# Routed experts write into seven DRAM regions of their own, summed on VectorE, in place of one accumulated region

## The chip, the core and the metric

The kernel runs on one NeuronCore of a Trainium2 chip. The metric is the device time of one execution in microseconds (us). The engines are TensorE (PE, matmuls; PEld its weight loads), VectorE (DVE), ScalarE (ACT), GpSimd (POOL) and SyncE (SP), each with its own queue of instructions, which it works off in order; they wait for one another on semaphores. SP issues plain DMAs. GpSimd issues the indirect ones, whose row numbers lie in a tile. All data is float32 unless a row says otherwise.

## The reference

Two transformer blocks on x of 8 batches x 512 tokens x 128 channels. Block 0 has attention and then a mixture of experts; block 1 has windowed attention and another feed-forward part. The change lies in the mixture of experts (`h` is the normalised, modulated x, `gb` a gate of batch and channel):

```
N = B * S                      # 4096 tokens
k = max(4, ceil(N * 2.0 / E))  # 1024 rows for each of E = 8 experts
xt = x.reshape(N, D)
scores = softmax(xt @ Wr)
G, idx = top_k(scores.T, k)    # per expert: the 1024 tokens that score highest
X_in = xt[idx]
h = gelu(einsum('ekd,edh->ekh', X_in, W1) + b1[:, None, :], approximate=False)
X_e = einsum('ekh,ehd->ekd', h, W2) + b2[:, None, :]
out = zeros((N, D)).at[idx.reshape(-1)].add((G[..., None] * X_e).reshape(E * k, D))
x = x + gb * out
```

A token may be chosen by several experts, so the sum over experts is part of the result. Within one expert every token stands at most once.

## The kernel before

**Stages.** The program has three: attention of block 0 (to about 459 us), the experts (function `moe`, to about 713) and block 1. X, the running activations, stays in SBUF as 32 tiles of 128 tokens. Attention leaves in DRAM `d_tab` (a token's 128 normalised channels and its 8 scores) and `d_hT` (the transposed rows).

**Expert 0 is dense.** It computes all 4096 tokens in four chunks of 1024 and weighs each token with its score or zero (`gate0`). Experts 1 to 7 are routed. The order is `ITS = (0, 0, 0, 1, 2, 3, 4, 5, 6, 7, 0)`: three dense chunks, the routed experts, the last dense chunk. `rx` is the expert's number less 1, `LOOP = 3`, `NR = 7`.

**Threshold search.** While TensorE computes the first dense chunks, VectorE searches in 15 rounds for the score above which an expert has 1024 tokens. From it VectorE and TensorE make the row numbers: `onehot(rx)` (L1377 to L1386) writes a comparison matrix R on VectorE, `lists(rx)` (L1461) multiplies it out on TensorE, and `index(rx)` (L1391 to L1395) writes `idx`. Two experts are done ahead; the others are made two experts ahead inside the loop (`AHEAD = 2`), at the top of VectorE's turn.

**One routed expert.** GpSimd gathers 1024 rows of `d_tab` into XG by eight indirect DMAs of 128 rows (L1280). TensorE transposes them (L1469, `rows_T`), ScalarE copies them to XT, TensorE computes the first layer (L1482, 16 instructions), ScalarE applies gelu (L1614), TensorE the second layer (L1494), ScalarE copies and adds the bias (OT, L1623), TensorE transposes back (L1501, `outputs_T`, two groups of four), and VectorE multiplies by the scores into Y (L1427, two of them, h = 0 and 1). GpSimd scatters Y by eight indirect DMAs (L1290) into `d_acc`, adding to what is there. Since two experts may add to one row, the scatters of an expert wait until those of the expert before have landed (L1286). On GpSimd's queue stands gathers of rx + 2, scatters of rx, gathers of rx + 3 and so on.

**TensorE's order in a turn.** First layer of expert e (with `outputs_T` of the expert before, h = 1, inside it), `lists` for the expert two ahead (it waits for R), `rows_T` of the next expert, `gates` (L1531, three small products with the gates of one batch; VectorE copies them at L1435 to L1438), second layer, `outputs_T` of e, h = 0. The second layer overwrites the PSUM banks that VectorE's Y reads.

**Dense outputs.** ScalarE leaves the outputs of a dense chunk in YD (L1627). TensorE transposes them (L1511, `dense_outputs_T`) and VectorE adds them, times `gate0`, to X (L1411, `dense_outputs`). For the first three chunks this stands behind expert 7: six groups of four transposes in turn with six groups of four updates, since both halves share two PSUM banks.

**End of the stage.** SP waits for the last scatter to land and loads the first two batches of `d_acc` into AC (L1850, 256 KB each). VectorE's `first_rows` multiplies AC by the gate GG and adds it to X (L1839, L1840), takes the statistics, adds the last dense chunk, and drains. GpSimd, after its wait for the scatters, drains (L1301), takes the root (L1846, L1847), and VectorE begins block 1 with bxn (L2076). The other batches of `d_acc` are loaded and added on GpSimd in block 1 (L2205, L2206). `d_acc` was cleared by one DMA of 2 MB during attention (L1086), from `zrow`.

## Time and profile before

| | us |
|---|---|
| median of 3 runs | 979.48 (976.18 to 981.32) |
| the profiled execution | 979.78 |
| its span in the profile | 978.0 |
| TensorE busy | 824.1 (84%) |
| VectorE busy | 572.1 (58%) |
| ScalarE busy | 440.4 (45%) |
| GpSimd busy | 413.9 (42%) |
| mean granted clock of TensorE | 0.904 of full speed |

The profile is of one execution, and its times in rows count from the start of the span. Shares are means over three stages that differ; in the stage of the experts each engine has idle time that some other engine ends. A row of a timeline says start, duration, engine, line, operation, output <- inputs, shapes and count, and in brackets how long the engine was idle before and what ended that. PE's rows overlap a little, since matmuls are pipelined and their ends are modelled.

### The profile page before, as it was taken

What the parts mean: (1) busy time and instruction counts of PE and PEld (TensorE: products, weight loads), DVE (VectorE), ACT (ScalarE), POOL (GpSimd) and SP (SyncE); (2) the same over time, 40 slices, a digit from 0 to 9 for tenths busy, and PEclk for the clock granted to TensorE, in tenths of its full rate; (3) what the DMA queues carried; (4) which work ended last, traced back from release to release, by engine and by line L of the source; (5) the groups of instructions that cost most, each with busy time, mean ns of one, the idle gap of its engine ahead of it and who ended that gap; (6) DMA issues with size and microseconds to landing.
All of it is one profiled execution on the core that took longest, in us unless ns stands there. A gap on an engine that the chain in (4) does not pass through costs nothing.

```text
span 978.0 us, 16352 instructions
## 1 busy us (share of the span) xinstructions
PE 824.1 (84%) x5918; PEld 400.0 (41%) x5918; DVE 572.1 (58%) x1480; ACT 440.4 (45%) x710; POOL 413.9 (42%) x539
## 2 busy tenths in 40 slices
PE   4687999899898989895888999789856679999885
PEld 3223333343333333333343454334434346666554
DVE  3676676657676767635677333300486567777741
ACT  1003554445454545471323433333246567776641
POOL 6221012323232322030005688887535676885323
PEclk9657999889999999996899998889968899999987
DMA  4211344134433132122101232333300111111100
GB/s 126 67 42 34 86 129 96 36 99 139 98 59 97 55 98 60 43 87 87 44 0 35 43 45 43 45 44 34 48 22 1 23 23 24 34 24 24 33 13 22
DMA packets 69095, 52.89 MB, mean 54 GB/s; under 512 B 20624, under 2 KB 62040, under 8 KB 68440
## 3 DMA queue, kind: packets, MB, share of 16 engines
q1 hardware_dynamic: 59160, 44.28, 17.6%
q0 software_dynamic: 9856, 7.58, 5.6%
q8 instruction: 48, 0.79, 0.3%
q14 instruction: 31, 0.25, 0.1%
HBM read 31.76 MB, written 18.23 MB: 51 GB/s over the span
## 4 chain that ended last, share of the span: by engine, by line
PE 50%; DVE 17%; POOL 13%; issue 8%; DMA 6%; ACT 3%; SPq 1%; POOLq 1%; DVEq 0%; ACTq 0%
PE bank L404 8%; POOL d_acc L1290 7%; PE bank L387 7%; DVE MX L793 6%; PE ps_s L362 5%; POOL XG L1280 3%; PE b1ps L1946 3%; PE b1ps L1935 3%; PE bank L407 2%; PE ps_s L371 2%; PE b1ps L1908 2%; PE ps_o L1494 2%; PE b1ps L1959 2%; DMA Q<-d_q 2%; PE ps_h L1482 1%
## 5 line engine op out<-in xcount | busy, mean ns | idle before, releaser
L793 DVE TENSOR_REDUCE MX<-bank 128x1 f32<-128x512 f32 (+3 forms) x352 | 216.2, 638 | 85.9 <-PE bank L407 81.6
L578 ACT ACTIVATE PR<-ps_s 128x1024 f32<-128x1024 f32 x160 | 158.9, 1023 | 155.5 <-PE ps_s L371 89.9
L404 PE MATMUL bank<-K,Q 96*128 96x512 bf16 (+3 forms) x512 | 136.4, 327 | 31.5 <-DVE MX L793 16.6
L404 PEld LDWEIGHTS bank<-K,Q 96*128 96x128 bf16 x512 | 44.5, 102 | 153.8 <-DVE MX L793 112.9
L362 PE MATMUL ps_s<-Q,K 99*128 99x512 bf16 x320 | 97.4, 393 | 1.8 <-DMA Q<-d_m 1.8
L1290 POOL DMA_INDIRECT d_acc<-Y,idx x56 | 87.6, 1565 | 20.3 <-issue 16.5
L407 PE MATMUL bank<-maskT,identb 128*128 128x128 bf16 (+2 forms) x352 | 92.7, 263 | 0.0
L1494 PE MATMUL ps_o<-H,w 128*128 128x512 f32 x176 | 91.5, 672 | 0.0
L387 PE MATMUL bank<-PR,VE 128*32 128x512 f32 x640 | 90.4, 639 | 0.0
L1280 POOL DMA_INDIRECT XG<-d_tab,idx x56 | 54.0, 965 | 77.6 <-DVE idx L1395 61.2
L1614 ACT ACTIVATE H<-ps_h,b1T 128x512 f32<-128x512 f32 x88 | 60.4, 687 | 42.2 <-PE ps_h L1482 40.0
L919 POOL TENSOR_SCALAR ve<-mv 128x4 f32<-128x4 f32 x8 | 1.9, 234 | 177.0 <-DVE mv L658 177.0
L1427 DVE TENSOR_TENSOR Y<-ps_o,XG 128x512 f32<-128x512 f32 x14 | 9.7, 692 | 99.0 <-PE ps_o L1501 81.8
L2058 ACT ACTIVATE PT<-b1ps 128x512 f32<-128x512 f32 x64 | 38.2, 597 | 39.6 <-PE b1ps L1946 38.5
L1482 PE MATMUL ps_h<-XT,w 128*128 128x512 f32 x112 | 54.0, 606 | 0.6 <-ACT XT L1606 0.5
L1494 PEld LDWEIGHTS ps_o<-H,w 128*128 128x128 f32 x176 | 36.6, 215 | 42.7 <-issue 42.0
L2063 ACT ACTIVATE PB<-SU 128x512 f32<-128x512 f32 x64 | 40.1, 627 | 19.6 <-DVE SU L2125 19.3
L2194 POOL TENSOR_SCALAR bxn<-X,bmv,brs 128x128 f32<-128x128 f32 x56 | 47.7, 864 | 1.5
L1935 PE MATMUL b1ps<-KB,QT 64*32 64x512 f32 x512 | 36.6, 629 | 13.2 <-issue 9.2
L2125 DVE TENSOR_TENSOR SU<-b1ps,mxs 128x512 f32<-128x512 f32 x64 | 44.2, 691 | 2.2
L889 POOL TENSOR_SCALAR xn<-X,mv,rs 128x128 f32<-128x128 f32 x56 | 44.0, 801 | 1.5
L1946 PE MATMUL b1ps<-ident,PB 128*128 128x128 f32 x256 | 43.3, 293 | 0.0
(333 smaller groups left out, 1388.8 us busy)
## 6 DMA issues: line engine op xcount, KB each, us to landing
Q<-d_q SPq DMA_DIRECT2D x24, 384.0 KB
d_q<-qs SPq DMA_DIRECT2D x24, 128.0 KB, 2.3
X<-L_attn_x SPq DMA_DIRECT2D x8, 256.0 KB, 4.7
w<-L_ffn_W SPq DMA_DIRECT2D x8, 256.0 KB, 3.5
d_acc<-zrow SPq DMA_DIRECT2D x1, 2048.0 KB, 9.4
w<-L_ffn_W SPq DMA_DIRECT2D x1, 2048.0 KB, 9.4
AC<-d_acc SPq DMA_DIRECT2D x8, 256.0 KB, 2.8
y<-X SPq DMA_DIRECT2D x8, 256.0 KB, 2.3
```

Source lines behind the costliest of these rows:

```text
L362: last = nc.tensor.matmul(ps_s[half][:, 512 * hh:512 * hh + 512], K[b % QB][0:KM, P * i:P * i + P], Q[b % QB][0:KM, 4 * hg:4 * hg + 4, P * ...
L387: last = nc.tensor.matmul(ps_y[32 * j:32 * j + 32, :], VE[b % QB][:, i, :], PR[t % 2][:, j, :], start=(i == 0), stop=(i == g), tile_positi ...
L404: nc.tensor.matmul(ps_mx[G % 2][:, x * w:(x + 1) * w], Q[b % QB][0:KR, h, P * g:P * g + P], K[b % QB][0:KR, 0:w], start=(x == 0), stop=Fal ...
L407: nc.tensor.matmul(diag, identb[:, :], bc(maskT[:, :].unsqueeze(1), [P, len(hs), P]), start=False, stop=True, skip_group_check=True).then_ ...
L578: nc.scalar.activation(PR[t % 2][:, 2 * half:2 * half + 2, :], ps_s[half][:, :].rearrange("p (a f) -> p a f", a=2), ACT.Exp, scale=DH ** - ...
L793: nc.vector.tensor_reduce(MX[b % 2][:, c:c + len(hs)], ps_mx[G % 2][:, 0:len(hs) * w].rearrange("p (x w) -> p x w", w=w), AX_X, ALU.max).t ...
L1280: nc.gpsimd.indirect_dma_start(out=XG[rx % 4][:, k, :], out_offset=None, in_=g.d_tab, in_offset=bass.IndirectOffsetOnAxis(ap=idx[:, rx + 1 ...
L1290: nc.gpsimd.indirect_dma_start(out=g.d_acc, out_offset=bass.IndirectOffsetOnAxis(ap=idx[:, rx + 1, k:k + 1], axis=0), in_=Y[rx % 2][:, k, ...
L1482: T_.matmul(ps_h[u % 2][:, :], g.w1[:, e, P * c:P * c + P], rows[:, 512 * h:512 * h + 512], start=True, stop=True).then_inc(h_ps, 1)
L1494: last = T_.matmul(ps_o[h][:, :], g.w2[:, ITS[it], c, :], H[h][:, c, :], start=(c == 0), stop=(c == NC_DI - 1))
L1935: last = T_.matmul(ps_s[(U + hh) % SB][32 * j:32 * j + 32, :], QT[b % 2][64 * hh:64 * hh + 64, q:q + 32], KB[b % 2][64 * hh:64 * hh + 64, ...
L1946: last = T_.transpose(ps_t[:, P * k:P * k + P], PB[U % 3][:, P * k:P * k + P], ident[:, :])
```

## The change

**Regions.** `d_acc` and its clearing in attention go. There are seven DRAM tensors `d_reg[0..6]` of 2 MB, cleared in a row by SP at the start of the expert stage, behind the loads of the dense chunks. The scatters of rx write `d_reg[rx]` with no add, and wait for no other expert's scatters; the first waits for the clearing. Their semaphore is split into two, for even and odd rx.

**Sums.** `part[b]`, one per batch, is made of free SBUF space (YD of the first three chunks and XD[2]). SP loads region 0 straight into it once its scatters have landed. For regions 1 to 5 it loads 256 KB at a time into the two buffers of AC, and VectorE adds each to `part[b]` (`add_region`); `sum_rd` counts the adds and frees the buffer. `add_region(rx - 1)` stands at the end of VectorE's turn rx, for rx of 2 to 6. Behind the last turn `add_sums` multiplies each part by GG and adds it to X, eight times two operations. Region 6 takes the path of `d_acc`: it is the one that `first_rows` and GpSimd add.

**Dense outputs.** Since YD is needed, the transposes and updates of the first three dense chunks move from behind expert 7 to before expert 1, on TensorE and on VectorE; the counts of the semaphores follow.

```diff
-    d_acc = dram("d_acc", [NB * T, D], F32)
+    d_reg = [dram(f"d_reg{i}", [NB * T, D], F32) for i in range(NE - 1)]
...
-                    if n == 0:
-                        sp.dma_start(d_acc.rearrange("(i p) d -> p i d", p=P),
-                                     bc(zrow[:, :].unsqueeze(1), [P, NTILE, D])).then_inc(s_lw, 16)
...
-    g.d_acc = d_acc
+    g.d_reg, g.d_acc = d_reg, d_reg[NE - 2]
...
+    part = [YD[:, T * b:T * b + T] for b in range(2 * LOOP)] + [XD[2][:, 0:T], XD[2][:, T:2 * T]]
+
+    def scattered(eng, rx):
+
+        eng.wait_ge(scat[rx % 2], 16 * NS * (rx // 2 + 1))
...
         def scatters(rx):
-            if rx >= 1:
-                pool.wait_ge(scat, 16 * NS * rx)
+            if rx == 0:
+                pool.wait_ge(zeroed, 16 * NR)
             for k in range(NS):
                 if k % 4 == 0:
-                    pool.wait_ge(y_rdy, 2 * rx + k // 4 + 1)
-                nc.gpsimd.indirect_dma_start(out=g.d_acc, out_offset=bass.IndirectOffsetOnAxis(ap=idx[:, rx + 1, k:k + 1], axis=0),
-                                             in_=Y[rx % 2][:, k, :], in_offset=None,
-                                             compute_op=ALU.add).then_inc(scat, 16)
+                    pool.wait_ge(y_rdy, 2 * LOOP + 2 * rx + k // 4 + 1)
+                nc.gpsimd.indirect_dma_start(out=g.d_reg[rx], out_offset=bass.IndirectOffsetOnAxis(ap=idx[:, rx + 1, k:k + 1], axis=0),
+                                             in_=Y[rx % 2][:, k, :], in_offset=None).then_inc(scat[rx % 2], 16)
...
+        def add_region(rx):
+            if rx == 1:
+                dve.wait_ge(first_in, 16 * NB)
+            for b in range(NB):
+                k = NB * (rx - 1) + b
+                dve.wait_ge(sum_in[k % 2], 16 * (k // 2 + 1))
+                if rx >= 2:
+                    dve.wait_ge(sum_rd, k - NB + 1)
+                V.tensor_tensor(part[b], part[b], g.AC[k % 2][:, :, :].rearrange("p i d -> p (i d)"), ALU.add
+                                ).then_inc(sum_rd, 1)
+
+        def add_sums():
+            dve.wait_ge(sum_rd, NB * (NR - 2))
+            for b in range(NB):
+                p3 = part[b].rearrange("p (i d) -> p i d", d=D)
+                lk(V.tensor_tensor(p3, p3, bc(g.GG[:, b:b + 1, :], [P, T // P, D]), ALU.mult))
+                Xb = g.X[:, T // P * b:T // P * b + T // P, :]
+                V.tensor_tensor(Xb, Xb, p3, ALU.add)
+
+        for c in range(LOOP):
+            dense_outputs(c)
...
             V.scalar_tensor_tensor(g.WVG[:, j, :], gate[2], 0.5, g.WT[:, 2, :], ALU.mult, ALU.mult).then_inc(gg_cp, 1)
+            if rx >= 2:
+                add_region(rx - 1)
+        add_sums()
         g.first_rows(dve)
...
         mix_weights_T()
+        for c in range(LOOP):
+            for h in range(2):
+                dense_outputs_T(c, h)
         for h in range(2):
             rows_T(0, h)
...
-        sp.wait_ge(scat, 16 * NS * NR)
+        for rx in range(NR):
+            sp.dma_start(g.d_reg[rx].rearrange("(i p) d -> p i d", p=P), bc(g.zrow[:, :].unsqueeze(1), [P, NTILE, D])
+                         ).then_inc(zeroed, 16)
+        for rx in range(NR - 1):
+            scattered(sp, rx)
+            for b in range(NB):
+                rows = g.d_reg[rx][T * b:T * b + T, :].rearrange("(i p) d -> p i d", p=P)
+                if rx == 0:
+                    if b == 0:
+                        sp.wait_ge(oT_ps, 2 * LOOP)
+                    sp.dma_start(part[b].rearrange("p (i d) -> p i d", d=D), rows).then_inc(first_in, 16)
+                    continue
+                k = NB * (rx - 1) + b
+                if k >= 2:
+                    sp.wait_ge(sum_rd, k - 1)
+                sp.dma_start(g.AC[k % 2][:, :, :], rows).then_inc(sum_in[k % 2], 16)
+        scattered(sp, NR - 1)
+        sp.wait_ge(sum_rd, NB * (NR - 2))
         g.first_loads(sp)
```

VectorE's queue at the turn of expert 3 and the start of the turn of expert 4, before. Y is expert 3's output, GG to WVG the gate copies, ohA to R the one-hot of expert 6, lst to idx its index:

```order
L1427 TENSOR_TENSOR Y<-ps_o,XG 128x512 [waits m_gathered2_1,m_out_transposed]
L1435 COPY GG<-ps_l 128x128 [waits p_gates_ps]
L1436 TENSOR_TENSOR WPG<-ps_l,w_proj 128x128
L1437 TENSOR_TENSOR BPG<-ps_l,b_proj 128x128
L1438 SCALAR_TENSOR_TENSOR WVG<-ps_l,WT 128x128
L1377 TENSOR_TENSOR ohA<-stile,kval 128x256
L1379 TENSOR_TENSOR A<-ohA,iota 128x32x8 [waits dve_chain]
L1380 TENSOR_SCALAR A<-ohA,iota_p 128x32x8
L1386 TENSOR_TENSOR R<-ps_r,slotf 128x4096 [waits m_list_ps,dve_chain]
```

The same place after, from the last gate copy on:

```order
L1460 SCALAR_TENSOR_TENSOR WVG<-ps_l,WT 128x128
L1427 TENSOR_TENSOR YD<-YD,AC 128x512 [waits m_region_rows0,m_first_region]
L1427 TENSOR_TENSOR YD<-YD,AC 128x512 [waits m_region_rows1]
L1427 TENSOR_TENSOR YD<-YD,AC 128x512 [waits m_region_rows0]
L1427 TENSOR_TENSOR YD<-YD,AC 128x512 [waits m_region_rows1]
L1427 TENSOR_TENSOR YD<-YD,AC 128x512 [waits m_region_rows0]
L1427 TENSOR_TENSOR YD<-YD,AC 128x512 [waits m_region_rows1]
L1427 TENSOR_TENSOR XD<-XD,AC 128x512 [waits m_region_rows0]
L1427 TENSOR_TENSOR XD<-XD,AC 128x512 [waits m_region_rows1]
L1381 TENSOR_TENSOR ohA<-stile,kval 128x256
L1383 TENSOR_TENSOR A<-ohA,iota 128x32x8 [waits dve_chain]
```

Eight adds, each with a wait for a load, now stand between the gate copies and the one-hot of expert 6. The same happens one turn later, for expert 7.

SP's queue of the same stage after; before, the loads of AC at the end came directly behind the dense loads (XD):

```order
L1679 DMA XD<-d_hT 128x1024 [waits a0_h_st]
L1681 DMA d_reg<-zrow 128x32x128 x7
L1690 DMA YD<-d_reg 128x4x128 [waits m_out_transposed,m_scattered0]
L1690 DMA YD<-d_reg 128x4x128 x5
L1690 DMA XD<-d_reg 128x4x128 x2
L1695 DMA AC<-d_reg 128x4x128 [waits m_scattered1]
L1695 DMA AC<-d_reg 128x4x128
L1695 DMA AC<-d_reg 128x4x128 [waits m_sums_read] x6
L1695 DMA AC<-d_reg 128x4x128 [waits m_sums_read,m_scattered0]
```

Of the eight loads of region 1 two are issued without a wait for an add; each of the other six waits for one. From region 2 on all eight do.

## Rows read from the trace of the kernel before

**Rows 1.** Page, costliest groups: count | busy us, mean ns | idle before, releaser.
```profile
L1290 POOL DMA_INDIRECT d_acc<-Y,idx x56 | 87.6, 1565 | 20.3 <-issue 16.5
L1427 DVE TENSOR_TENSOR Y<-ps_o,XG 128x512 f32<-128x512 f32 x14 | 9.7, 692 | 99.0 <-PE ps_o L1501 81.8
```
**Rows 2.** GpSimd's timeline: start us, duration us, line, operation [idle before].
```profile
546.12 0.94 POOL L1280 DMA_INDIRECT XG<-d_tab,idx  x1 [0.30 <-issue]
...
554.87 1.63 POOL L1290 DMA_INDIRECT d_acc<-Y,idx  x1 [0.31 <-issue]
556.81 1.57 POOL L1290 DMA_INDIRECT d_acc<-Y,idx  x1 [0.30 <-issue]
...
580.03 1.62 POOL L1290 DMA_INDIRECT d_acc<-Y,idx  x1 [0.30 <-issue]
```
**Rows 3.** Chain of waits at the end of the experts: start us, us, what.
```profile
701.65 3.30 DMA d_acc<-Y,idx
704.98 7.09 POOLq L1301
```
**Rows 4.** TensorE's timeline: first output transposes of experts 1 to 7, one list.
```profile
552.66 0.60 PE L1501 MATMUL ps_o<-ident,OT 128*128 128x128 f32 x4
...
573.84 0.60 PE L1501 MATMUL ps_o<-ident,OT 128*128 128x128 f32 x4
...
583.68 0.97 PE L1461 MATMUL ps_l<-A,R 128*128 128x16 bf16 x32 [1.44 <-DVE R L1386]
...
596.66 0.60 PE L1501 MATMUL ps_o<-ident,OT 128*128 128x128 f32 x4
...
644.20 0.60 PE L1501 MATMUL ps_o<-ident,OT 128*128 128x128 f32 x4
...
668.50 0.60 PE L1501 MATMUL ps_o<-ident,OT 128*128 128x128 f32 x4
...
684.67 0.60 PE L1501 MATMUL ps_o<-ident,OT 128*128 128x128 f32 x4
```
**Rows 5.** VectorE's and TensorE's timelines: dense updates, last chunk's first layer.
```profile
687.70 5.25 DVE L1411 SCALAR_TENSOR_TENSOR X<-ps_o,gate,X 128x128 f32<-128x128 f32 x20
...
692.88 8.60 PE L1482 MATMUL ps_h<-XD,w 128*128 128x512 f32 x16
```
**Rows 6.** VectorE's timeline at the end of the stage.
```profile
707.73 0.69 DVE L1839 TENSOR_TENSOR AC<-AC,GG 128x512 f32<-128x512 f32 x1 [4.46 <-DMA AC<-d_acc]
...
710.38 2.13 DVE L1411 SCALAR_TENSOR_TENSOR X<-ps_o,gate,X 128x128 f32<-128x128 f32 x8
713.68 3.08 DVE L2076 TENSOR_SCALAR bxn<-X,bmv,brs 128x128 f32<-128x128 f32 x4 [1.17 <-POOL brs L1847]
```
**Rows 7.** Clearing on the page; landings of AC's loads in the tile's view.
```profile
d_acc<-zrow SPq DMA_DIRECT2D x1, 2048.0 KB, 9.4
...
DMA to landing us min/median/max: 2.6/2.8/4.5
```
**Rows 8.** VectorE's timeline: one-hot preparation, the second Y, the one-hot.
```profile
512.84 0.42 DVE L1377 TENSOR_TENSOR ohA<-stile,kval 128x256 f32<-128x256 int32 x1
...
555.46 0.69 DVE L1427 TENSOR_TENSOR Y<-ps_o,XG 128x512 f32<-128x512 f32 x1 [1.46 <-PE ps_o L1501]
...
556.86 0.41 DVE L1377 TENSOR_TENSOR ohA<-stile,kval 128x256 f32<-128x256 int32 x1
...
558.03 4.42 DVE L1386 TENSOR_TENSOR R<-ps_r,slotf 128x4096 bf16<-128x4096 f32 x1
```
**Rows 9.** Windows, two second layers: stretch, us, busy by engine, PEclk, DMA, GB/s.
```profile
586.96:596.82 9.86, 9.86 (x19) 4.32 (x19) 0.00 (x0) 0.69 (x1) 8.03 (x7) 0.72 0.37 36
609.19:616.32 7.13, 7.13 (x19) 3.25 (x19) 0.00 (x0) 0.69 (x1) 6.18 (x4) 1.00 0.41 37
```
**Rows 10.** SP's timeline: the last two loads of dense chunks.
```profile
460.99 1.95 SPq L1654 DMA_DIRECT2D XD<-d_hT  x2
```
**Rows 11.** View of tile XG: duration min/median/max, first and last start.
```profile
L1280 POOL DMA_INDIRECT XG<-d_tab,idx x56: 940/947/1243, 521.0 to 654.3; - x56
```

39 lines of the change are left out of this document (18 added, 21 removed).

## The prediction

> **What bounds the kernel now.** I read the page first, then the GpSimd timeline of the expert stage, then the chain of waits, and last the VectorE and TensorE timelines of the same stretch. The page gives GpSimd 56 scatters at 1565 ns [rows 1]. The timeline shows them back to back with the 56 gathers: a gather every 1.25 us, a scatter with add every 1.86 us, and the first scatters of two experts 25.2 us apart (554.87 to 580.03) [rows 2], which is 8 x 1.25 + 8 x 1.86 = 24.9. The chain of waits passes through them and through the landing of the last scatter to 704.98, then through GpSimd's drain (7.09 us) [rows 3]. Call a turn the time from the first output transposes of one expert to those of the next. The six turns are 21.2, 22.8, together 47.5 for the next two, then 24.3 and 16.2, 132.0 in all [rows 4]. So the first two turns are TensorE's own pace; GpSimd's lag makes itself felt only in turns 4 and 5, where expert rows come late. The scatter is the bound of only part of the stage, and a gain must be read turn by turn.
>
> **What goes away.** A scatter without add is not in this trace. Its nearest rows are the gather (step 1.25) and the scatter with add (1.86) [rows 2]; I take 1.25, since it also writes 128 descriptors for 512-byte rows and reads nothing at its destination. That frees 56 x 0.61 = 34 us of GpSimd, and the wait for the scatters of the expert before goes too. Where GpSimd is no longer late it is worth nothing more: at 1.25 or at 1.86 the sum below moves by 1 us at most, in the tail. A turn without GpSimd's lag is TensorE's: 21.2 to 22.8 with a list, 17.1 without (16.2 [rows 4] and an estimated 0.9 for the eight transposes of rows that turn 6 has not).
>
> **Front: the dense transposes move.** Six groups of four transposes and the 24 updates of X stood after expert 7 and now stand before expert 1. VectorE's update sets their pace, 5.25 us for 20 [rows 5], 1.05 per group of four; the sixth group begins five such steps after the first and takes 0.5 to 1.1. Expert 1 therefore starts about 5.5 us later. At the old place they took as long between expert 7 and the last dense chunk; but there TensorE's gain buys nothing, since VectorE will be later (tail).
>
> **Middle: a wait stands ahead of the one-hot.** This is the large term. After experts 3 to 7 VectorE adds the region of the expert before: eight loads of 256 KB through two buffers, an add after each. VectorE works in order, and what is queued behind are the one-hot and the index of a later expert. TensorE waits for that one-hot before it goes on to the second layer.
> An add of 128x512 from SBUF is the 0.69 of the row on AC [rows 6], 0.72 with its start. A load takes 2.76 from its issue (704.97, the end of the chain's scatter) to VectorE's start at 707.73 [rows 3, 6]; the landings of such loads are 2.6, 2.8 and 4.5 at least, median and most [rows 7]. Two loads are in ahead. Load 3 is issued only when add 1 is done, about 0.1 later, so each further pair costs 0.1 + 2.76 + 0.69 = 3.55: a region takes 2 x 0.72 + 3 x 3.6 = 12.2. These rows come from a queue without scatters in it; beside gathers and scatters I take 3.0 instead of 2.76, hence r = 12.9 per region.
> Only the one-hots of experts 6 and 7 stand behind a region. In those two turns: 3.5 from the output transposes to the end of the second Y (552.66 to 556.15), 0.7 for gate copies, 12.9 for the region, 5.6 for the one-hot (556.86 to 562.45) [rows 4, 8], and from the list to the next output transposes 13.0 (583.68 to 596.66) [rows 4]. That last figure is a turn in which the clock had fallen after a wait: the second layer took 9.86 at a granted clock of 0.72, against 7.13 at 1.00 [rows 9]; after a wait of some 13 us I take the slow one. Sum 35.7, twice 71.4 against 47.5: **+23.9**.
> Turn 5 has no list: TensorE 17.1, VectorE 3.5 + 0.7 + 12.9 = 17.1, against 24.3: **-7.2**. Turn 6 stays 16.2 for TensorE, with VectorE 0.9 behind. Turns 1 and 2 keep their 44.0. Middle together +16.7.
>
> **Tail: VectorE ends last.** From the last expert's output transposes (684.67) to the first normalisation of the next stage (713.68) it is 29.0 now [rows 4, 6]. After: 2.5 to the end of both Y, 0.7 gate copies, 12.9 for the sixth region, 0.9 for the last gate copies, 16 operations of 0.72 for the gated sums = 11.5, then the part that stood there before, first rows 2.65 (707.73 to 710.38) and X updates 2.13 [rows 6], and 0.3 to the start: 33.6. TensorE's last chunk needs 8.6 for its first layer [rows 5] and 7.1 for the second [rows 9], near 20 with gates and transposes, and hides. GpSimd's drain of 7.09 [rows 3] hides too. Tail **+4.6**. If a scatter keeps 1.86, region 6 comes about 1 us later.
>
> **Zeroing.** One clearing of 2 MB (9.4 us to landing [rows 7]) leaves the attention stage, where no engine waits for it: at nothing, up to 1 us of gain. Seven are issued behind SP's last dense load, near 463 [rows 10], with nothing that is needed soon behind them on SP: 7 x 9.4 = 66 us, to 529. Their cover is the threshold search; they are needed at the first scatter, 554.87 + 5.5 = 560. The gathers of expert 1 start at 521 [rows 11] and share the last 8 us with them; TensorE now asks for those rows 5.5 later, which is their margin. Cost nothing; if the cover is gone, a few us (rival 4).
>
> **Sum.** 5.5 + 16.7 + 4.6 = 26.8. The profiled execution took 979.8 (span 978.0, 1.8 around it), 0.3 above the median of 979.5: 979.8 + 26.8 = **1006.6, forecast 1007**.
>
> **A rule against this change.** Around VectorE's one-hot preparation, which reads two SBUF tensors, GpSimd is in scatters: 0.41 beside them (556.86), 0.42 in a stretch without any (512.84) [rows 8]; the add of SBUF on SBUF should keep its 0.69. The Trainium skill, page "SBUF — State Buffer", section "Who interferes with whom", says that a VectorE instruction with two SBUF inputs contends with a GpSimd instruction that reads SBUF, and the later one blocks for all of the other's time. By that rule 40 adds beside gathers and scatters would wait; the trace's one pair of rows does not bear it out.
>
> **Rivals.**
> (1) Adds on time. If all loads of a region were in before VectorE asks, r = 8 x 0.72 = 5.8. The sum falls by three regions (turns 3, 4 and the tail; turns 5 and 6 are then TensorE's): 26.8 - 3 x 7.1 = 5.5, **985**. Against it: load 3 cannot be issued before add 1 is done.
> (2) The other side, faster: the region's sum fits in VectorE's idle time and nothing waits for it, with GpSimd's lag gone. Place: between gate copies and one-hot. With r = 0 the sum is 26.8 - 38.7 = -11.9, **968**. The sign turns at r = 12.9 - 26.8 / 3 = 4.0, that is 0.5 us for load and add together; the add alone measures 0.69. For it: VectorE idles 99 us before the 14 Y now [rows 1]. Against it: that idle time lies behind the one-hot, the sum stands before it.
> (3) Loads slowed by gathers and scatters. All five regions lie on the path then. Landings of 3.6 give r = 14.7 and +9, **1016**; 4.5 (the longest seen) gives r = 17.4 and +22, **1029**.
> (4) Zeroing collides. 14.7 MB keep the DMA engines full through the threshold search. If it takes more than 560 - 463 = 97 us, the first scatter waits; if gathers of expert 1 land after 539, TensorE does. Price 3 to 10: **1010 to 1017**.
> (5) Port lock. A GpSimd gather is under way for 0.94 of each 1.25 us [rows 2]; an add would wait 0.4 on average, four adds in series per region, five regions: +8, **1015**.
>
> **How the numbers follow.** Forecast 0.64, with its own spread: landings of 2.6 (-4), clock kept high in the two long turns (-3), front 5 to 6.5, landings of 3.3 (+5), so 998 to 1013. Rival 1 0.05, rival 2 0.03, rival 3 0.13, rival 4 0.07, rival 5 0.06; 0.02 for what I have not seen. 996 to 1024 leaves out rivals 1 and 2 and the far half of 3, about 0.16. A measurement of this kernel can tell about 0.5% (5 us) from no change: faster 0.04 (rival 2), within it 0.02, slower 0.94.
>
> **What would show it.** In the changed kernel: scatters at a step near 1.25; TensorE idle some 13 us before the lists of experts 6 and 7, ended by R; VectorE's adds in pairs, each second one after about 2 us of waiting for a load; turns of 35 to 36 twice, then 17 and 17; the X updates before expert 1, whose output transposes come near 558; the end of VectorE's part about 33 us after expert 7's. I am wrong if the adds follow each other without waits (rival 1), if the one-hots of experts 6 and 7 don't hold TensorE (rival 2), or if the adds are longer than 0.7 (rival 5).

## The result, and the profile after

The changed kernel took **1023.5 us** (1020.6 to 1030.3, 4 runs), beside 979.1 us of the kernel before: ratio 1.0465, 95% interval 1.0403 to 1.0527. Forecast were 1007 us in a range of 996 to 1024: the direction was right and the size too small, a ratio of 1.028 against 1.0465. In us the median lies at the upper edge of the range, as a ratio (1024 over 979.5 is 1.0454) just above it. The profiled execution took 1020.6 us, its span is 1018.8.

The page of the changed kernel (count | busy us, mean ns | idle before, releaser; at the end DMA issues, KB, us to landing) answers [rows 1] and [rows 7]:

```profile
L1284 POOL DMA_INDIRECT XG<-d_tab,idx x56 | 53.4, 953 | 134.8 <-DVE idx L1399 119.6
L1294 POOL DMA_INDIRECT d_reg<-Y,idx x56 | 56.8, 1015 | 36.8 <-DVE Y L1452 20.9
L1452 DVE TENSOR_TENSOR Y<-ps_o,XG 128x512 f32<-128x512 f32 x14 | 9.6, 691 | 64.5 <-PE ps_o L1524 44.8
d_reg<-zrow SPq DMA_DIRECT2D x7, 2048.0 KB, 17.4
AC<-d_reg SPq DMA_DIRECT2D x48, 256.0 KB, 2.9
```

A scatter without add holds GpSimd 1015 ns, as against 1565 in [rows 1]. (L1284 and L1294 are the gathers and scatters, L1452 is Y, L1524 the output transposes, L1486 the list.) TensorE's timeline (start us, us, engine, line, operation [idle before <- what ended it]) answers [rows 4], again with the first output transposes of experts 1 to 7 (L1524), and ahead of them the dense transposes (L1536) at their new place:

```profile
524.50 0.60 PE L1536 MATMUL ps_o<-ident,YD 128*128 128x128 f32 x4
531.36 1.12 PE L1536 MATMUL ps_o<-ident,YD 128*128 128x128 f32 x4 [6.26 <-issue]
537.36 2.15 PE L1536 MATMUL ps_o<-ident,YD 128*128 128x128 f32 x8 [4.88 <-DVE X L1415]
...
541.63 1.64 PE L1494 MATMUL ps_x<-ident,XG 128*128 128x128 f32 x8
...
560.74 0.60 PE L1524 MATMUL ps_o<-ident,OT 128*128 128x128 f32 x4
...
567.34 1.10 PE L1507 MATMUL ps_h<-XT,w 128*128 128x512 f32 x2 [2.13 <-ACT H L1639]
571.46 2.07 PE L1507 MATMUL ps_h<-XT,w 128*128 128x512 f32 x2 [3.02 <-issue]
575.01 3.78 PE L1507 MATMUL ps_h<-XT,w 128*128 128x512 f32 x4 [1.48 <-ACT H L1639]
...
588.75 0.60 PE L1524 MATMUL ps_o<-ident,OT 128*128 128x128 f32 x4
...
616.07 0.60 PE L1524 MATMUL ps_o<-ident,OT 128*128 128x128 f32 x4
...
639.38 1.02 PE L1486 MATMUL ps_l<-A,R 128*128 128x16 bf16 x32 [6.60 <-DVE R L1390]
...
653.12 0.60 PE L1524 MATMUL ps_o<-ident,OT 128*128 128x128 f32 x4
...
675.98 1.02 PE L1486 MATMUL ps_l<-A,R 128*128 128x16 bf16 x32 [14.46 <-DVE R L1390]
...
690.19 0.60 PE L1524 MATMUL ps_o<-ident,OT 128*128 128x128 f32 x4
...
707.23 0.60 PE L1524 MATMUL ps_o<-ident,OT 128*128 128x128 f32 x4
...
723.39 0.60 PE L1524 MATMUL ps_o<-ident,OT 128*128 128x128 f32 x4
```

The turns are 28.0 and 27.3, then 37.1 and 37.1, then 17.0 and 16.2. The two long ones have the length that was forecast. In the second TensorE waits 14.46 us for R. In the first it waits only 6.60, since its own first layer is late there, but VectorE's queue sets the length all the same. VectorE's timeline shows what TensorE waits for: the region's adds, at first in pairs with 2.3 to 2.4 us of waiting for a load between them, then one by one with shorter waits (three more adds in rows left out here), and the one-hot of expert 6 behind them:

```profile
620.69 1.29 DVE L1427 TENSOR_TENSOR YD<-YD,AC 128x512 f32<-128x512 f32 x2
624.26 1.49 DVE L1427 TENSOR_TENSOR YD<-YD,AC 128x512 f32<-128x512 f32 x2 [2.29 <-DMA AC<-d_reg]
628.16 0.69 DVE L1427 TENSOR_TENSOR YD<-YD,AC 128x512 f32<-128x512 f32 x1 [2.41 <-DMA AC<-d_reg]
...
633.72 0.42 DVE L1381 TENSOR_TENSOR ohA<-stile,kval 128x256 f32<-128x256 int32 x1
```

From 620.69 to 633.80, the end of the last add, a region takes 13.1. What was not forecast is the rest: 28.0 and 27.3 in the turns that should have kept their 44.0 together, and 35.1 us from the first one-hot (506.49) to the transposes of expert 1's rows (541.63), which had taken 19.7. ScalarE's and VectorE's timelines of that stretch say who waits:

```profile
523.38 0.78 ACT L1652 ACTIVATE YD<-ps_o,b2g,gbT 128x512 f32<-128x512 f32 x1 [7.42 <-remote]
530.53 0.78 ACT L1652 ACTIVATE YD<-ps_o,b2g,gbT 128x512 f32<-128x512 f32 x1 [6.38 <-remote]
533.35 0.49 ACT L1666 ACTIVATE WT<-ps_l 128x384 f32<-128x384 f32 x1 [2.04 <-remote]
```
```profile
521.94 0.17 DVE L1395 COPY lst<-ps_l 128x16 f32<-128x16 f32 x1 [3.87 <-remote]
...
536.18 2.16 DVE L1415 SCALAR_TENSOR_TENSOR X<-ps_o,gate,X 128x128 f32<-128x128 f32 x8 [12.70 <-remote]
```

All five read what TensorE writes, and all wait long after TensorE's row has ended: X starts at 536.18, although the first four transposes are recorded at 524.50 and the other four at 531.36. The profile sees the semaphore change at the moment of release, but no instruction that would have changed it ("remote"). I call these **delays**. The last such wait ends at 630.0; from the one-hot of turn 3 on the kernel runs as forecast.

### The profile page after: what moved, and what is told of

It is laid out like the page before. It is cut to its first block, busy times and chain, and to the rows that moved or that the text cites. A ratio compares the mean times of both kernels' runs of the same rounds, so it can differ in the third digit from the quotient of the medians.

```text
span 1018.8 us, 16497 instructions
## 1 busy us (share of the span) xinstructions
PE 818.5 (80%) x5918; PEld 398.9 (39%) x5918; DVE 609.0 (60%) x1536; ACT 440.5 (43%) x710; POOL 381.3 (37%) x539
## 3 DMA queue, kind: packets, MB, share of 16 engines
q0 software_dynamic: 3584, 7.58, 2.6%
## 4 chain that ended last, share of the span: by engine, by line
PE 48%; DVE 21%; issue 14%; DMA 8%; ACT 2%; POOL 2%; SPq 2%; another core or an unknown queue 2%; DVEq 0%; POOLq 0%; ACTq 0%
PE bank L404 7%; PE bank L387 7%; DVE MX L793 6%; PE ps_s L362 5%; DMA AC<-d_reg 3%; PE b1ps L1988 3%; PE ps_o L1517 3%; PE b1ps L1977 3%; PE bank L407 2%; PE b1ps L2001 2%; PE ps_s L371 2%; DMA Q<-d_q 2%; DVE R L1390 2%; PE b1ps L1950 2%
## 5 line engine op out<-in xcount | busy, mean ns | idle before, releaser
L404 PE MATMUL bank<-K,Q 96*128 96x512 bf16 (+3 forms) x512 | 133.6, 321 | 34.3 <-DVE MX L793 17.8
L1284 POOL DMA_INDIRECT XG<-d_tab,idx x56 | 53.4, 953 | 134.8 <-DVE idx L1399 119.6
L362 PE MATMUL ps_s<-Q,K 99*128 99x512 bf16 x320 | 94.8, 384 | 2.2 <-DMA Q<-d_m 2.2
L387 PE MATMUL bank<-PR,VE 128*32 128x512 f32 x640 | 88.0, 623 | 0.0
L1517 PE MATMUL ps_o<-H,w 128*128 128x512 f32 x176 | 85.6, 636 | 0.0
L1507 PE MATMUL ps_h<-XT,w 128*128 128x512 f32 x112 | 63.8, 689 | 17.3 <-ACT H L1639 12.3
L1294 POOL DMA_INDIRECT d_reg<-Y,idx x56 | 56.8, 1015 | 36.8 <-DVE Y L1452 20.9
L1452 DVE TENSOR_TENSOR Y<-ps_o,XG 128x512 f32<-128x512 f32 x14 | 9.6, 691 | 64.5 <-PE ps_o L1524 44.8
## 6 DMA issues: line engine op xcount, KB each, us to landing
d_reg<-zrow SPq DMA_DIRECT2D x7, 2048.0 KB, 17.4
```

Source lines behind the costliest of these rows:

```text
L362: last = nc.tensor.matmul(ps_s[half][:, 512 * hh:512 * hh + 512], K[b % QB][0:KM, P * i:P * i + P], Q[b % QB][0:KM, 4 * hg:4 * hg + 4, P * ...
L387: last = nc.tensor.matmul(ps_y[32 * j:32 * j + 32, :], VE[b % QB][:, i, :], PR[t % 2][:, j, :], start=(i == 0), stop=(i == g), tile_positi ...
L404: nc.tensor.matmul(ps_mx[G % 2][:, x * w:(x + 1) * w], Q[b % QB][0:KR, h, P * g:P * g + P], K[b % QB][0:KR, 0:w], start=(x == 0), stop=Fal ...
L1294: nc.gpsimd.indirect_dma_start(out=g.d_reg[rx], out_offset=bass.IndirectOffsetOnAxis(ap=idx[:, rx + 1, k:k + 1], axis=0), in_=Y[rx % 2][:, ...
L1507: T_.matmul(ps_h[u % 2][:, :], g.w1[:, e, P * c:P * c + P], rows[:, 512 * h:512 * h + 512], start=True, stop=True).then_inc(h_ps, 1)
L1517: last = T_.matmul(ps_o[h][:, :], g.w2[:, ITS[it], c, :], H[h][:, c, :], start=(c == 0), stop=(c == NC_DI - 1))
```

## What was tested

Theory at first (A): the seven clearings, 14.7 MB in the same stretch, cause the delays. Rival (B): the scatters without add. Each group below ran beside its own runs of the kernel before. Stretches are read from each profile: *front*, first one-hot to the first transposes of XG; turns as in the prediction; *tail*, expert 7's output transposes to TensorE's first ones of the next stage; *stage*, first one-hot to those. "Remote" counts idle stretches of ScalarE and VectorE between 500 and 760 us that the profile ends with that word.

```
kernel (group)                    time   before  remote  front  turns1+2  3+4   5     6     tail  stage
before (of the record)            979.8  979.5     0     19.7    44.0     47.5  24.3  16.2  32.2  202.9
before (3)                        983.8  981.2    11     18.5    45.1     50.8  17.0  16.2  35.1  205.1
changed (of the record)          1023.5  979.1    11     35.1    55.3     74.1  17.0  16.2  36.1  253.0
changed (2)                      1020.9  984.4     5     34.1    52.1     73.1  17.0  16.2  36.0  248.3
changed (4)                       999.2  977.0     0     23.4    44.0     74.5  17.0  16.2  36.4  230.1
changed (5)                      1004.9  978.3     0     23.4    44.0     74.0  17.0  16.2  36.1  229.4
clearings early (1)              1002.0  977.7     0     23.4    44.0     74.0  17.0  16.2  35.8  229.0
clearings early (3)              1025.0  981.2     5     25.1    55.6     73.3  17.0  16.2  36.3  245.6
sums behind the index (1)         974.6  977.7     0     25.1    45.6     45.4  17.0  16.2  35.8  203.8
sums behind the index (3)        1001.3  981.2    11     34.2    55.7     52.0  17.0  16.2  35.9  230.4
before + 7 clearings (1)          976.1  977.7     0     19.7    44.0     47.5  24.3  16.2  32.3  203.0
before, no add (1)                960.7  977.7     0     19.7    44.0     39.2  17.0  16.2  30.4  185.5
before, dense first (2)           991.6  984.4    11     34.0    43.3     51.0  17.9  16.2  35.7  217.8
sums interleaved (2)              995.6  984.4    12     34.2    53.1     50.5  17.0  16.2  29.8  220.1
sums interleaved (3)              991.3  981.2     8     25.1    51.0     52.7  17.0  16.2  30.0  214.1
changed, one wait (4)            1002.2  977.0     0     25.1    45.6     74.7  17.0  16.2  36.4  233.7
changed, both waits (5)          1001.6  978.3     0     23.4    44.0     75.1  17.0  16.2  36.2  230.6
interleaved, one wait (4)         970.9  977.0     0     23.4    44.0     42.3  17.8  16.2  33.2  195.5
interleaved, one wait (5)         968.2  978.3     0     23.4    44.0     42.3  17.3  16.2  33.2  195.1
```

(Times are medians of the group's runs; the first row's is its profiled execution. "Before" is the median of the kernel before in the same group. Stretches and "remote" are of one profiled execution each. Groups 1 and 2 ran on one chip, groups 3, 4 and 5 on one each. The kernel with three load buffers, group 2, is told below.)

### Group 1: the four parts

**Clearings early.** The seven clearings go out one per batch in the attention stage, and the first scatter's wait for them goes:

```diff
+                    if n < NE - 1:
+                        sp.dma_start(d_reg[n].rearrange("(i p) d -> p i d", p=P),
+                                     bc(zrow[:, :].unsqueeze(1), [P, NTILE, D])).then_inc(s_lw, 16)
...
-        for rx in range(NR):
-            sp.dma_start(g.d_reg[rx].rearrange("(i p) d -> p i d", p=P), bc(g.zrow[:, :].unsqueeze(1), [P, NTILE, D])
-                         ).then_inc(zeroed, 16)
```

> The changed kernel with its seven clearings issued earlier, one for each batch in the attention stage, behind the late weights, instead of all seven at the start of the expert stage; nothing else differs. Theory A (the 14.7 MB of clearing that run through the threshold search and on into the first expert are what delays TensorE's hand-overs there): the stretch from the one-hot of expert 1 to its first row transposes falls from 35.1 back to about 25 us (19.7 before plus the 5.5 of the moved transposes), turns 1 and 2 fall from 28.0 and 27.3 to 22, together about -20, so about 1000 us. Theory B (the delays come from the scatters without add, or from gathers and scatters in one unbroken run on GpSimd): the delays stay, 1020 within 5. The attention stage may lengthen by up to 9 us if its own loads meet the clearings.

Measured 1002.0 us, ratio 1.0272 (1.0201 to 1.0343), with no delays. Taken alone this confirmed A.

**Sums behind the index.** A region is summed one turn later, behind the one-hot and the index:

```diff
                     index(rx + AHEAD)
+                if rx >= 3:
+                    add_region(rx - 2)
...
+            else:
+                add_region(NR - 2)
...
-            if rx >= 2:
-                add_region(rx - 1)
```

> The changed kernel with the sum of a region put behind the one-hot and the index of the same turn on VectorE (one turn later than before), so that nothing which TensorE asks for stands behind the eight waits for loads; the region of the expert before last is summed in the last turn. Same loads, same adds. Theory A (the region's 13.1 us ahead of the one-hot is what makes turns 3 and 4 37 us long): these two fall to 22 to 26 each, 22 to 30 us less in all, partly given back in turn 5 and the tail, so 995 to 1000 us. Rival B (the turns are long because the loads themselves or the scatters hold TensorE): turns 3 and 4 stay above 33, 1015 to 1022.

Measured 974.6 us, ratio 0.9968 (0.9923 to 1.0012). Turns 3 and 4 fall from 74 to 45.4 us: theory A of this run is right on the 37-us turns. But the time fell by 20 more than that, and this kernel clears its regions exactly as the changed one does, without delays in its front. That speaks against the clearings.

**The kernel before with seven clearings** of spare tensors, at the place where the changed kernel has them:

```diff
+        for rx in range(NR):
+            sp.dma_start(g.d_spare[rx].rearrange("(i p) d -> p i d", p=P), bc(g.zrow[:, :].unsqueeze(1), [P, NTILE, D])
+                         ).then_inc(zeroed, 16)
```

> The kernel before, plus seven clearings of 2 MB each of spare DRAM tensors that nothing reads, issued by SP at the start of the expert stage as the changed kernel does. Theory A (the clearing traffic delays TensorE's hand-overs around expert 1): the stretch from the one-hot of expert 1 to its first row transposes grows from 19.7 to about 30 and turns 1 and 2 by some 5 each, so 990 to 1000 us. Theory B (clearing is hidden, as predicted): 979 within 3.

Measured 976.1 us, ratio 1.0011 (0.9971 to 1.0050); stage 203.0 us against 202.9. Its windows (us, busy by engine, PEclk, DMA share, GB/s) show the DMA engines full through the threshold search, and nobody waits for them:

```profile
460.00:500.00 40.00, 33.79 (x96) 14.90 (x96) 29.13 (x170) 12.45 (x18) 0.00 (x0) 1.00 1.01 301
```

Clearings alone bring no delays and cost nothing. Whether delays need them this run can't say; the kernels without them in groups 2 and 3 can.

**The kernel before with scatters that don't add** (the sum over experts of a row is left out):

```diff
-                                             in_=Y[rx % 2][:, k, :], in_offset=None,
-                                             compute_op=ALU.add).then_inc(scat, 16)
+                                             in_=Y[rx % 2][:, k, :], in_offset=None).then_inc(scat, 16)
```

> The kernel before with its 56 scatters writing instead of adding, still one behind the other's completion for each expert; a row chosen by several experts then keeps only the last one's part, so the sum over experts is left out. Theory (scatter step falls from 1.86 to 1.27, GpSimd is no longer late in turns 4 and 5): these turns fall from 27 and 24 to 22 and 17 and the time to 965 to 970 us. Rival (plain scatters back to back with gathers delay TensorE's hand-overs in turns 1 and 2, as in the changed kernel): turns 1 and 2 grow from 21 and 23 to 27 or so, and the time stays at 975 to 982.

Measured 960.7 us, ratio 0.9855 (0.9786 to 0.9924). Turns 4 and 5 shrink from 28.0 and 24.3 to 19.7 and 17.0, the first three stay: what the add costs is 17 us, 15.6 of them in the turns that [rows 4] showed long and the rest in the tail. Plain scatters alone bring no delays. GpSimd's row on its page:

```profile
L1290 POOL DMA_INDIRECT d_acc<-Y,idx x56 | 55.2, 985 | 31.2 <-issue 15.9
```

### Groups 2 and 3: the delays follow the time of the run, not the kernel

> The changed kernel once more, unaltered, next to the others of this group. The kernel with the sums behind the index has the same program up to turn 3, yet its first row transposes come 25.1 us after the first one-hot (35.1 in the changed kernel's profile) and its first turns take 22.8 and 22.9 (28.0 and 27.3). Theory C (the extra 20 us belong to the moment or the chip on which the changed kernel was first run, not to its program): no such delays here, front 23 to 26, turns 22 to 23, time 1000 to 1005 us. Theory D (they belong to the program): 1018 to 1030 again, with turns of 27 to 28.

Measured 1020.9 us, ratio 1.0377 (1.0326 to 1.0428), with delays; taken alone it spoke for D.

**Three load buffers** for the regions instead of two (`sum_in[k % 3]`, `g.AC[k % 3]`, loads wait for add k - 3):

> The changed kernel with three load buffers for the regions instead of two, so that a third load is on its way while VectorE adds; nothing else differs. By the sum (a pair of loads costs 0.1 + 2.76 + 0.69 = 3.55 us) three loads now share that: a region falls from 13.1 to about 9 us, on the path three times (turns 3, 4 and the tail): 10 to 12 us less than the changed kernel run beside it. Rival (the loads' own throughput sets the pace of 1.6 us each, not the number of buffers): less than 3 us.

Measured 1005.7 us, ratio 1.0202 (1.0154 to 1.0251), against 1020.9 of the changed kernel beside it: 15 us less, where 10 to 12 were expected. Its profile is of its slowest run (1015.9), so I use only lengths inside it: turns 3 and 4 take 65.2 us against 73.1 and the tail 32.0 against 35.9, which is 11.8 of the 15; the rest stays open. A region takes 10.1 us from 628.01 to 638.15, and the waits for R fall from 14.8 and 14.5 to 11.6 and 10.4. VectorE's timeline now has three adds in a row, then one wait:

```profile
628.01 1.94 DVE L1427 TENSOR_TENSOR YD<-YD,AC 128x512 f32<-128x512 f32 x3
631.86 0.69 DVE L1427 TENSOR_TENSOR YD<-YD,AC 128x512 f32<-128x512 f32 x1 [1.91 <-DMA AC<-d_reg]
```

So the number of buffers sets r, as the sum's 3.6 per pair had it, though 10.1 is more than the 9 expected.

**Sums interleaved**: sums behind the index, and in the last turn each batch's gated addition right behind its last add:

```diff
                                 ).then_inc(sum_rd, 1)
+                if gated and b < NB - 1:
+                    dve.wait_ge(sum_rd, k + 1)
+                    add_sums(b)
```

> The kernel with the sums behind the index, and in the last turn each batch's gated addition to X (two operations of 0.69 us) done right behind that batch's last region sum, in the 1.0 to 1.1 us that VectorE waits there for the next load, instead of all sixteen after them. Tail from the last expert's output transposes from 35.8 to about 28 us: region 13.0 plus gated sums 11.3 = 24.3 us become 8 x 2.2 = 17.6. So 966 to 969 us, against 974.6 without this step and 977.7 for the kernel before. Rival (TensorE's last dense chunk or GpSimd's drain then ends last): 970 to 973.

Measured 995.6 us, ratio 1.0111 (1.0075 to 1.0147). The tail did what was expected (29.8 instead of 35.8), yet the kernel was 21 us slower than its parent in group 1, with the same program up to the last turn: delays again, from 533 us on.

**The kernel before with the dense transposes first**, that part of the change alone:

> The kernel before with the one part of the change alone that moves the transposes and updates of the first three dense chunks ahead of expert 1; scatters still add into one array, one clearing, no regions. The prediction put this at +5.5 us for the front. Expected: front 25.2 instead of 19.7 us, turns as before, and the tail (29.0, then 32.2 to the first transposes of the next stage) unchanged since GpSimd's last scatter sets it: 983 to 984 us. Rival (the transposes fill time in which TensorE waited at the tail, and their absence there gives some back): 978 to 981.

Measured 991.6 us, ratio 1.0088 (1.0050 to 1.0125), with delays and a front of 34.0. As a measure of the 5.5 us it is inconclusive. That it has delays, with one clearing and scatters that add, shows that neither the seven clearings (A) nor plain scatters (B) are needed for them.

Group 3 repeated four kernels to separate time from program:

> The kernel before, unaltered, for a profile beside the others of this group. In the second group of runs it took 984.4 us, in the first 977.7, and every kernel of the second group showed TensorE's results 2 to 8 us late around expert 1 (34 us from the first one-hot to the first row transposes), while none of the first group did (19.7, or 23 to 25 with the dense transposes in front). Theory C (the delays belong to the time of the run, on any kernel whose dense transposes stand there or not): if the three others show them, this one shows a milder form, 983 to 987 us. Theory D (they belong to each program): no delay here, 977 to 980 us.

> The changed kernel with its seven clearings in the attention stage, once more. Theory C (the delays belong to the time of the run): if they come, front 34 us, turns 1 and 2 at 24 to 28, 1018 to 1024 us, like the changed kernel in the second group; if not, 1000 to 1005. Theory D (they belong to the program, and this one has none): 1000 to 1005 us whatever the others do.

> The changed kernel with the sums behind the index, once more. Theory C: if the delays come, 995 to 1003 us, above the one with interleaved sums by some 7; if not, 975 again. Theory D: 975 again, although the next kernel, the same program up to its last turn, takes 995.

> The kernel with the sums behind the index and the gated additions between the last region's sums, once more. Theory C: 7 to 8 us below the kernel without the interleaving, whatever the level of both: 967 to 969 without the delays, 993 to 998 with them. Theory D: 995 again, 20 above its neighbour.

Measured 983.8, 1025.0, 1001.3 and 991.3 us, ratios 1.0008 (0.9964 to 1.0053), 1.0455 (1.0390 to 1.0521), 1.0192 (1.0113 to 1.0271) and 1.0085 (1.0035 to 1.0136), all four with delays. The unchanged programs of group 1 went from 1002 to 1025 and from 975 to 1001. Theory C holds: the delays belong to the time of the run. Groups 1 and 2 ran on the same chip, one without and one with them, so it isn't the chip alone either. That holds for the profiled executions; the kernel before took 969.5 to 985.5 us in group 1 and 973.6 to 995.5 in group 3, so its single times don't tell which of them had delays. Even the kernel before has them, in VectorE's timeline:

```profile
534.72 0.17 DVE L1391 COPY lst<-ps_l 128x16 f32<-128x16 f32 x1 [6.14 <-remote]
```

but it loses only some 2 us of its stage (205.1 against 202.9). From expert 1's output transposes to the next stage both profiles take the same 164.2 us: GpSimd's scatters end that stretch, and a late TensorE costs nothing in it.

### Groups 4 and 5: do GpSimd's long runs bring them on?

In the changed kernel's profile the delays lie inside GpSimd's unbroken runs of sixteen gathers and scatters (513.5 to 533.4, 552.9 to 572.8, 580.5 to 600.5, 607.9 to 628.3) or end within 3 us behind one, and none lies beside its later runs of eight. Two kernels break the runs up. One wait:

```diff
+            for h in range(2):
+                pool.wait_ge(gat[rx % 4][h], 16 * 4 * (rx // 4 + 1))
```

Both waits: that, and `scattered(pool, rx)` behind each expert's scatters.

> The changed kernel, unaltered, to show in which condition this group runs: with the delays 1018 to 1026 us (front 34 to 35 us, turns 1 and 2 at 24 to 28), without them 1000 to 1005 (front 23 to 25, turns 21 to 23).

> The changed kernel, with GpSimd waiting for each expert's eight gathers to land before it goes on to the scatters (some 2.4 us), so that it never issues sixteen in one run. Theory E (unbroken runs of sixteen bring TensorE's delays on): in a group with delays, the front falls from 34 to about 26 us and turns 1 and 2 from 28 to 23, so 1003 to 1008 us beside 1020 of the changed kernel. Theory F (the length of the runs has nothing to do with it): 1018 to 1026 like its neighbour. In a group without delays both are the same within 3 us.

> The kernel with the sums behind the index and the gated additions interleaved, with the same wait for landed gathers. Theory E: in a group with delays, 972 to 978 us where without the wait it took 991 and 996; that would be below the kernel before (981 to 984 there). Theory F: 990 to 997. In a group without delays: 967 to 972.

Measured 999.2, 1002.2 and 970.9 us, ratios 1.0235 (1.0154 to 1.0316), 1.0231 (1.0158 to 1.0305) and 0.9933 (0.9904 to 0.9963).

> The changed kernel, unaltered, to show in which condition this group runs: with TensorE's delays 1018 to 1026 us, without them 998 to 1003.

> The changed kernel with GpSimd waiting for the landing of each eight gathers and of each eight scatters before it issues the next, so that it has no run longer than eight. Theory E (runs of sixteen bring the delays on): in a group with delays 1003 to 1010 us, at least 10 below its neighbour, no semaphore of TensorE later than 0.3 us. Theory F (the length has nothing to do with it): within 4 us of its neighbour. In a group without delays: 0 to 5 us above the neighbour, since GpSimd's turn grows from 20.3 to about 25 us and a gather may come late in turns 1 and 2.

> The kernel with sums behind the index, gated additions interleaved, and the wait for landed gathers, once more: without delays 971 again, 6 us below the kernel before; with them 985 to 993 by theory F, 975 to 980 by theory E.

Measured 1004.9, 1001.6 and 968.2 us, ratios 1.0275 (1.0219 to 1.0330), 1.0238 (1.0184 to 1.0291) and 0.9919 (0.9879 to 0.9960).

Neither group had delays, so E and F weren't told apart; only that the waits cost 3 us or less. Long runs are at least not sufficient: the changed kernel of group 4 has one of forty DMAs (542.4 to 593.0, pauses under 1.3 us not counted) without a delay. Nor is a run of sixteen necessary: in group 3's kernel with early clearings the first gathers go out as two runs of eight (526.4 to 536.4 and 538.7 to 548.5), and four delayed waits end between 537.8 and 550.1.

What the two groups do give is the changed kernel without delays. TensorE's and ScalarE's timelines of group 4, for the rows shown above, and TensorE's return from its wait in turn 3:

```profile
526.19 1.36 PE L1536 MATMUL ps_o<-ident,YD 128*128 128x128 f32 x8
528.01 0.66 PE L1536 MATMUL ps_o<-ident,YD 128*128 128x128 f32 x4 [0.46 <-DVE X L1415]
...
531.60 1.04 PE L1494 MATMUL ps_x<-ident,XG 128*128 128x128 f32 x8
...
552.84 5.81 PE L1507 MATMUL ps_h<-XT,w 128*128 128x512 f32 x12
...
617.24 1.02 PE L1486 MATMUL ps_l<-A,R 128*128 128x16 bf16 x32 [14.63 <-DVE R L1390]
...
621.57 9.97 PE L1517 MATMUL ps_o<-H,w 128*128 128x512 f32 x16
```
```profile
522.63 0.78 ACT L1652 ACTIVATE YD<-ps_o,b2g,gbT 128x512 f32<-128x512 f32 x1 [5.83 <-PE ps_o L1517]
526.07 0.78 ACT L1652 ACTIVATE YD<-ps_o,b2g,gbT 128x512 f32<-128x512 f32 x1 [2.65 <-PE ps_o L1517]
```

Twelve matmuls of a first layer stand in one block of 5.81 us, where the delayed profile has them in pieces from 563 to 579. By medians the change costs 22.2 us in group 4 and 26.6 in group 5, beside 44.4 in the record.

**A kernel faster than before.** Sums behind the index, gated additions interleaved, one wait for landed gathers: 0.7% and 0.8% below the kernel before in groups 4 and 5. VectorE's timeline in the last turn of group 5 has no wait for a load left between the region's sums, here the first two:

```profile
678.82 0.68 DVE L1429 TENSOR_TENSOR YD<-YD,AC 128x512 f32<-128x512 f32 x1
679.54 0.69 DVE L1437 TENSOR_TENSOR YD<-YD,GG 128x512 f32<-128x512 f32 x1
680.26 0.69 DVE L1439 TENSOR_TENSOR X<-X,YD 128x512 f32<-128x512 f32 x1
680.87 0.68 DVE L1429 TENSOR_TENSOR YD<-YD,AC 128x512 f32<-128x512 f32 x1
```

With delays it wasn't run; without its wait it was then 1.1% and 0.9% slower than the kernel before.

## Why the prediction was right and wrong

Against the changed kernel **without delays** (group 4, stage 230.1 against 202.9: +27.2) the sum of 26.8 stands nearly term by term. Against the run of the record (253.0: +50.1) it misses 23 us, and these lie in two steps.

- **Front, forecast +5.5.** +3.7 or +5.4 (23.4 or 25.1) without delays, by whether a short fall of the clock lies in it: the twelve second-layer matmuls ahead of the dense transposes take 5.40 us in the one and 7.09 in the other. +15.4 in the record. **This is one of the two steps that failed:** 11.7 us of late results (35.1 against 23.4) lie on top of the transposes.
- **Turns 1 and 2, "keep their 44.0".** 44.0 without delays, 55.3 in the record: **the other step that failed,** 11.3 us. The sentence behind both, that a turn without GpSimd's lag is TensorE's own pace of 21.2 to 22.8, took TensorE's pace in one execution for a constant and put late results at nothing. What makes them late stays open.
- **Turns 3 and 4, 71.4.** 74.5 and 74.0, 74.1 in the record: the mechanism is right, the size 3 us short. r was 12.9 and measured 13.1 to 13.3; the stretch from the list to the next output transposes, 13.0 in the sum, took 14.1 (617.24 to 631.37, group 4). The second layer there is as slow as the sum took it (9.97 us, 9.86 in [rows 9]), but the lower clock (half of full from 606.8 to 627.3) now covers the row transposes and gates ahead of it too, 4.3 us from the list to the second layer against 3.3. Sums behind the index took 29 us off these two turns and 27 off the time inside group 1 (974.6 against 1002.0 with early clearings), which shows that the wait ahead of the one-hot made them long.
- **Turns 5 and 6, 17.1 and 16.2.** 17.0 and 16.2, in every profile of the changed kernel. In turn 5 the region just fits: Y of expert 6 starts at 686.37 (group 4), right behind the last add, with no wait between.
- **Tail, +4.6.** From expert 7's output transposes to bxn 33.1 in group 4 (701.90 to 735.03) and 32.8 in the record, against 29.0: +4.1 and +3.8. Right.
- **Zeroing at nothing.** Right in size: seven clearings in the kernel before, 976.1 against 977.7. Its landing was mis-sized, 17.4 us in the queue where the sum had 9.4; the transfers overlap, and the DMA engines were free again by about 510, not 529 (their busy share is 0.65 from 505 to 510 and 0.01 from 510 to 515 in the record).
- **Scatter without add, 1.25.** 1.27 per scatter (560.27 to 561.54 in group 4). The reason given, that both write 128 descriptors, the trace doesn't show: GpSimd's queue moved the same 7.58 MB in 9856 packets before and in 3584 after.
- **Rival 1 and 2** (loads on time, nothing waits): not here, but what they turn on is real. With three buffers r fell to 10.1, and moving the sum off TensorE's path was worth 27 us.
- **Rival 3** (loads slowed by the scatters): no, the median of 48 landings was 2.9 in group 4. **Rival 4**: no. **Rival 5**, with the rule of the Trainium skill, page "SBUF — State Buffer", section "Who interferes with whom": no. The adds, with two SBUF inputs, took 0.68 to 0.73 us each, all 40, though 26 of them overlapped a gather or scatter (as at 620.69 and 624.26 above, inside GpSimd's run of 607.9 to 628.3). No block for the whole of a gather or scatter, 0.94 or more, is seen. The same section says that its probe saw no such stall between `tensor_tensor` and DMA issue, and with that the trace agrees.

What the range lacked is a term for exposure. In the kernel before GpSimd's queue covers TensorE from expert 1's output transposes on, so a late TensorE costs it 2 us of the stage and 3 to 7 in all (977.0 to 978.3 in the groups without delays, 981.2 and 984.4 in those with them). The change takes GpSimd off the path and puts TensorE, VectorE and the dense transposes on it one behind the other; delays then cost 18 to 23 us (230.1 to 248.3 and 253.0). All four runs of the record have the length that goes with delays; the kernel before, at 979, lay where both conditions look alike.

Also unforecast, and no effect of the change: in the record's profile the expert stage starts 9.0 us earlier than before (450.4 against 459.3). Profiles of the kernel before with an edit behind that point started it at 450.3 and 453.3. The first one-hot comes 7.5 us earlier (506.49 against 514.02) and what follows the stage takes 1.8 less, so that the stage's +50.1 shows as +40.8 in the whole span.

## What to carry to other kernels

A turn that another engine's lag covers hides how much its own engine varies: before a change takes that cover away, compare several executions of the engine that becomes the bound, not one. Loads that are summed through two buffers cost their latency once per pair; put such a sum behind whatever another engine waits for, give it a third buffer, and let independent work stand between its waits. And when a result and one undone part agree, run the unchanged kernel once more beside it: here the first group "proved" a wrong cause by 21 us. Count a profile's semaphore records against what the program's DMAs must leave before reading much into its waits.

## What the runs showed of the hardware

**TensorE's results can come late, in some executions and not in others.** In the eleven profiles without delays, ScalarE and VectorE have not one idle stretch ended by "remote" between 500 and 760 us; in the nine others 5 to 12 of them, 16 to 55 us in all, the first at 521.9 and the last at 664.8. The granted clock doesn't tell: in the delayed stretch from 519 to 529 of the record it is at full (2.4 GHz), and falls to the lower level (1.2 GHz) only at 529.2, for 13.7 us. It shows in the windows of the two profiles (the same columns as above; PEclk is the third number from the end):

```profile
500.00:545.00 45.00, 31.12 (x150) 16.66 (x148) 24.94 (x57) 9.89 (x15) 15.40 (x16) 0.81 0.29 79
```
```profile
500.00:545.00 45.00, 40.59 (x217) 20.56 (x216) 30.16 (x63) 15.88 (x24) 17.34 (x19) 0.96 0.36 103
```

(the record's first, group 4's second). I can't tell whether the lower clock follows from TensorE's idling there or belongs to the cause.

**The same nine profiles have lost records of semaphores.** Each of the 112 gathers and scatters adds to its semaphore once per DMA engine, 16 times, 1792 in all. The eleven profiles without delays hold 1780 to 1790 of these changes, the nine with delays 584 to 1056 (629 in the record), although the DMA packets behind them are recorded in full in both (3584 on GpSimd's queue in the record and in group 4). Of the waits of ScalarE and VectorE between 500 and 760 us the profile leaves 19 to 27 without any releaser ("issue") in the nine, 3 in each of the eleven. So the recording was in another condition too, and "remote" and "issue" must be read with that in mind; that TensorE's results are late rests on the starts of the rows that read them, not on these words.

**The cause is open.** Ruled out as necessary: the clearings, the regions, scatters without add, the sums (the kernel before has delays without any of them), and runs of sixteen. Ruled out as sufficient: all of these, and long runs on GpSimd. Two readings are left that no run here decides.

The Trainium skill, page "TensorE: Matmul & The Clock Gate", section "Seeing it yourself", warns that the recorded clock events have been unreliable and that the engine has been seen stuck at a lower rate; the array would then be slower than its record. No single slower rate fits the rows, though. The two halves of a second layer, eight matmuls apart, reach ScalarE 7.15 us apart in the record (523.38 and 530.53) and 3.44 in group 4, but 3.55 in the delayed profile of the kernel before with the dense transposes first, as at full speed, while there the four short transposes behind them come 8 us late (recorded at 528.75, read at 537.45). ScalarE's and VectorE's timelines:

```profile
527.54 0.78 ACT L1626 ACTIVATE YD<-ps_o,b2g,gbT 128x512 f32<-128x512 f32 x1 [7.92 <-remote]
531.09 0.78 ACT L1626 ACTIVATE YD<-ps_o,b2g,gbT 128x512 f32<-128x512 f32 x1 [2.78 <-remote]
```
```profile
537.45 1.12 DVE L1411 SCALAR_TENSOR_TENSOR X<-ps_o,gate,X 128x128 f32<-128x128 f32 x4 [9.73 <-remote]
```

The other reading is the recording. A lost record looks like this in the record's VectorE timeline, where the same row one turn earlier still has its releaser:

```profile
692.98 0.69 DVE L1452 TENSOR_TENSOR Y<-ps_o,XG 128x512 f32<-128x512 f32 x1 [1.46 <-PE ps_o L1524]
...
710.02 0.69 DVE L1452 TENSOR_TENSOR Y<-ps_o,XG 128x512 f32<-128x512 f32 x1 [1.46 <-issue]
```

The Trainium skill, page "NOTIFIC — the notification-queue block", section "7.1 Overflow: three behaviours, one of which stalls the engine", says that the block which writes such records can, when a queue fills, either lose a record or hold back the engine that produces it. By the second, part of the delays would be the recording's own. The lost records fit the first and don't show the second, and every execution here was recorded, so the two can't be told apart.
